# Second unit's samples issued by ACT and SyncE together, its weights fetched from the first unit's second chunk on, its transposes and splits later in the pass

## What is computed

```python
def dense(x, wi, wo):                      # D = 256, F = 1024
    return relu(x @ wi) @ wo
s0 = dense(x, swi[0], swo[0]);  s1 = dense(x, swi[1], swo[1])
h  = relu(einsum('bsd,bdf->bsf', x, wi[label]))
eo = einsum('bsf,bfd->bsd', h, wo[label])
gate_in = concatenate([eo[:, 0], s0[:, 0], s1[:, 0]], axis=-1)
w  = softmax(relu(gate_in @ g1) @ g2, axis=-1)
x  = x + eo * w[0] + s0 * w[1] + s1 * w[2]
x  = x + zX * lap_x(x) + zY * lap_y(x) + zR * x * (1 - x)
```

## Time and profile before

| | us |
|---|---|
| median of 3 runs | 1149.19 |
| lowest, highest | 1147.92, 1150.12 |
| the profiled execution | 1148.16 |
| its span, first to last instruction | 1146.6 |
| TensorE busy in it | 1136.5 |
| VectorE, ACT, GpSimd busy | 676.5, 455.3, 78.8 |

### The profile page before, as it was taken

The page is one execution under the profiler, slowest core; times in us unless marked ns, Lnnn a source line. Parts: engine busy times, 40 slices in busy tenths (PEclk is TensorE's granted clock), DMA queues, the critical chain, the costliest instruction groups (busy, mean ns, idle before and its releaser), DMA issues.

```text
span 1146.6 us, 16856 instructions
## 1 busy us (share of the span) xinstructions
PE 1136.5 (99%) x6068; PEld 970.9 (85%) x6068; DVE 676.5 (59%) x1031; ACT 455.3 (40%) x806; POOL 78.8 (7%) x123
## 2 busy tenths in 40 slices
PE   8999999999999999999999999999999999999998
PEld 7788888888888888888888888888888888888888
DVE  5556666656666644556555655565465565556556
ACT  3455555555655532323333333333333233333323
POOL 2111212211111100000000000000000000000001
PEclk9999999999999999999999999999999999999999
DMA  9555556646565514023032131231230230221200
GB/s 284 148 154 178 168 173 199 187 145 202 179 186 156 161 33 119 15 70 73 22 73 45 48 75 25 59 83 22 63 83 17 68 78 16 73 47 47 75 29 24
DMA packets 111252, 111.83 MB, mean 98 GB/s; under 512 B 78441, under 2 KB 87234, under 8 KB 111170
## 3 DMA queue, kind: packets, MB, share of 16 engines
q1 hardware_dynamic: 96802, 59.78, 19.3%
q0 software_dynamic: 13952, 50.60, 14.6%
q10 hardware_dynamic: 416, 0.39, 0.1%
HBM read 89.40 MB, written 17.04 MB: 93 GB/s over the span
## 4 chain that ended last, share of the span: by engine, by line
PE 97%; DMA 1%; SPq 1%; issue 0%; DVE 0%; DVEq 0%
PE acc L919 31%; PE hbank L892 16%; PE hbank L891 16%; PE hbank L893 16%; PE acc L920 16%; PE tbank L845 1%; DMA xs<-in_x 1%; PE acc L905 0%; SPq L1228 0%; DMA rw<-in_L_cond_swi 0%; PE hbank L870 0%; PE tbank L840 0%; PE acc L930 0%; PE acc L932 0%; PE acc L931 0%
## 5 line engine op out<-in xcount | busy, mean ns | idle before, releaser
L579 DVE SCALAR_TENSOR_TENSOR hl<-hbank,hh 128x512 fp32r<-128x512 f32 (+2 forms) x440 | 275.7, 627 | 427.9 <-ACT hh L1030 427.3
L1030 ACT ACTIVATE hh<-hbank 128x512 fp32r<-128x512 f32 (+2 forms) x440 | 240.2, 546 | 588.8 <-PE hbank L893 585.9
L919 PE MATMUL acc<-swo,hh 128*128 128x512 f32 x992 | 359.3, 396 | 0.0
L920 PE MATMUL acc<-swo,hl 128*128 128x256 f32 x992 | 277.8, 280 | 0.0
L919 PEld LDWEIGHTS acc<-swo,hh 128*128 128x128 f32 x992 | 186.3, 188 | 43.7
L891 PE MATMUL hbank<-xh,swh 128*128 128x512 f32 (+1 forms) x528 | 205.3, 389 | 0.0
L892 PE MATMUL hbank<-xl,swh 128*128 128x512 f32 (+1 forms) x528 | 205.0, 388 | 0.0
L893 PE MATMUL hbank<-xh,swl 128*128 128x512 f32 (+1 forms) x528 | 202.1, 383 | 0.0
L920 PEld LDWEIGHTS acc<-swo,hl 128*128 128x128 f32 x992 | 187.1, 189 | 9.6
L919 PE MATMUL acc<-ewo,hh 128*128 128x512 f32 x528 | 194.9, 399 | 0.3
L920 PE MATMUL acc<-ewo,hl 128*128 128x256 f32 x528 | 148.0, 280 | 0.0
(11 more groups left out here) (194 smaller groups left out, 893.2 us busy)
## 6 DMA issues: line engine op xcount, KB each, us to landing
rw<-in_L_cond_wi POOLq DMA_DIRECT2D x44, 512.0 KB, 4.5
rw<-in_L_cond_wo POOLq DMA_DIRECT2D x44, 512.0 KB, 4.7
xs<-in_x SPq DMA_DIRECT2D x128, 64.0 KB, 3.2
eo_scratch<-eo SPq DMA_DIRECT2D x128, 64.0 KB, 2.7
xs<-in_x SPq DMA_DIRECT2D x16, 512.0 KB, 4.4
rw<-in_x SPq DMA_DIRECT2D x256, 32.0 KB, 2.3
ei<-eo_scratch SPq DMA_DIRECT2D x16, 512.0 KB, 5.5
out<-ot SPq DMA_DIRECT2D x15, 512.0 KB, 6.3
```

The costliest lines, as they stand in the source:

```text
L579: e.scalar_tensor_tensor(h_slot(HL, g), bank[:, 0:w], 0.0, h_slot(HH, g).bitcast(F32), ALU.max, ALU.subtract).then_inc(h_lo, 1)
L919: e.matmul(acc[j][:, 0:2 * D], HH[:, g % NH, js], woc[:, c, :], start=(c == 0), stop=False)
L920: m = e.matmul(acc[j][:, D:2 * D], HL[:, g % NH, js], woc[:, c, 0:D], start=False, stop=last)
L1030: e.activation(h_slot(HH, g), hbank[g % HRING][:, 0:w], ACT.Relu).then_inc(h_hi, 1)
```

## The change

1. `first_samples` on ACT issues seven samples: four of the first unit, then numbers 0, 1 and 2 of the second. SP issues four of the first and numbers 3 to 7 of the second, and no longer waits for the 12th first product.
2. GpSimd waits for the 18th first product, the one of chunk `(2, 1)`, before it fetches the second unit's weights.
3. The first half of the second unit's transposes, with its splits, moves from chunk `(2, 3)` to `(2, 4)`.
4. ACT splits the second unit's pieces 0, 2, 1, 3 after chunks 4, 5, 6, 7 instead of 2, 4, 5, 7 of pass 2; VectorE follows.
5. VectorE splits the first unit's piece 0 after chunk `(1, 6)` instead of `(1, 5)`.

```diff
-FIRST_BY = {"ACT": (0, 1, 2, 3), "SP": (4, 5, 6, 7)}
+FIRST_BY = {"ACT": ((1, 0), (1, 1), (1, 2), (1, 3), (2, 0), (2, 1), (2, 2)), "SP": ((1, range(4, 8)), (2, range(3, 8)))}
@@ tile_parts(n, c)
-    if c == 3:
+    if c == (4 if n == 2 else 3):
         return [(tile, 0 if big else None)]
     return [(tile, 1)] if c == 6 and big else []
@@
-FIRST_LOW = {(1, 5): [(2, 0)], (2, 0): [(2, 2)], (2, 2): [(2, 1)], (2, 4): [(2, 3)]}
+FIRST_LOW = {(1, 6): [(2, 0)], (2, 0): [(2, 2)], (2, 2): [(2, 1)], (2, 4): [(2, 3)]}
@@ unit_cuts(n, c)
-    at = {2: 0, 4: 2} if 2 <= n < 1 + NU and UNITS[n - 2][1] == 2 else {2: 0, 4: 2, 5: 1, 7: 3}
-    out = [(n + 1, at[c])] if 2 <= n < 1 + NU and c in at else []
+    out = []
+    if 2 <= n < 1 + NU:
+        at = {4: 0, 5: 2, 6: 1, 7: 3} if n == 2 else {2: 0, 4: 2} if UNITS[n - 2][1] == 2 else {2: 0, 4: 2, 5: 1, 7: 3}
+        if c in at:
+            out.append((n + 1, at[c]))
@@ first_samples() on ACT
                 e.wait_ge(dve_seq, AT["samples"])
-                for i, b in enumerate(FIRST_BY["ACT"]):
-                    e.reg_load(regs[i], tab[0:1, 0, b:b + 1])
+                e.wait_ge(x0_prod, 1)
+                for i, (tile, b) in enumerate(FIRST_BY["ACT"]):
+                    slot = slots_of(tile - 1)[0] + b
+                    e.reg_load(regs[i % 4], tab[0:1, 0, slot:slot + 1])
...
@@ GpSimd
             e.wait_ge(h_prod, 12)
             load_unit(0, (2, 1, 3))
+
+            e.wait_ge(h_prod, 18)
             for u in range(1, NU):
                 load_unit(u, (0, 2, 1, 3))
@@ load_unit_x(u, part) on SP
                 if tile == 2:
                     e.wait_ge(x0_prod, 1)
-                    e.wait_ge(h_prod, 12)
@@ SP
-            load_unit_x(0, FIRST_BY["SP"])
-            load_unit_x(1)
+            for tile, part in FIRST_BY["SP"]:
+                load_unit_x(tile - 1, part)
```

More of the change, by code:

```diff
@@ L1066, in first_samples @@
                 e.wait_ge(dve_seq, AT["samples"])
-                for i, b in enumerate(FIRST_BY["ACT"]):
-                    e.reg_load(regs[i], tab[0:1, 0, b:b + 1])
-                    v = e.snap(regs[i], min_val=0, max_val=NS - 1)
-                    e.dma_start(XS[1][b:128:8, :, :], x[bass.ds(v, 1), :, :].rearrange("a (p j) d -> (a p) j d", p=16)) \
-                        .then_inc(x_in[1], 16)
+                e.wait_ge(x0_prod, 1)
+                for i, (tile, b) in enumerate(FIRST_BY["ACT"]):
+                    slot = slots_of(tile - 1)[0] + b
+                    e.reg_load(regs[i % 4], tab[0:1, 0, slot:slot + 1])
+                    v = e.snap(regs[i % 4], min_val=0, max_val=NS - 1)
+                    e.dma_start(XS[tile % 2][b:128:8, :, :],
+                                x[bass.ds(v, 1), :, :].rearrange("a (p j) d -> (a p) j d", p=16)) \
+                        .then_inc(x_in[tile % 2], 16)
             def quadratic(t):
```

## The result

| | before | after |
|---|---|---|
| median of 7 runs (us) | 1147.92 | 1144.82 |
| lowest, highest | 1147.42, 1150.12 | 1143.1, 1145.5 |
| span of the profiled execution | 1146.6 | 1142.8 |

The ratio after / before is 0.9967 (95% interval 0.9955 to 0.9978): 3.8 us of 1148, between 2.5 and 5.2. It compares the means of the seven runs, 1148.32 and 1144.51; the medians of the table lie 3.1 us apart. The profiled spans differ by the same 3.8 us. 4.2 us and 1145.0 were predicted. That 1144.82 lies so near to 1145.0 is in part luck: the prediction started from 1149.19, the median of three runs, and with four more runs the median before is 1147.92.

What follows compares the result with a forecast made beforehand. TensorE, busy for 99% of the span, was taken to bound the kernel. Wait 2.70 plus low clock 1.76 minus 0.3 for the first unit's samples gave 4.2 us saved: 1149.19 to 1145.0 us, range 1143.4 to 1148.0.

Steps and rivals of the forecast that it cites:

- The wait and its price: TensorE's wait at the second unit's transposes costs 2.70 us, the low clock after it 1.76 us; both go.
- The clock's term: From the second unit's transposes to the next chunk, 4.99 us at the low clock against 3.23 at full: 1.76 us.
- The samples: SyncE's last issue for the second unit comes at 20.6 instead of 24.96 and lands by 27.9.
- The shift itself is worth nothing.: Second unit's transposes moved from fourth to fifth chunk cost the same there; TensorE asks for the samples at 31.98.
- The first unit's samples: In the opening, ACT's three extra transfers delay them; 0.3 us of loss taken, between 0 and 1.9 us.
- Rival A: First unit's samples land 1.9 us later, TensorE idles 2.7 us there, the clock falls; 1148.4 us, chance 0.11.
- Slack of the weights: The second unit's first weight piece lands between 31.1 and 38.6 and may land by 40.5 without cost: zero.
- The count of the chain behind the first piece: Splits, ReLU and VectorE's work after the second unit's first weight piece take 4.0 us, due at 44.5.
- VectorE, ACT, the small loads: VectorE's fuller load, ACT's three extra issues and SyncE's small loads behind the samples each cost zero.
- B: The wait goes, but the clock still falls somewhere in the opening; 1146.8 us, chance 0.07.
- C: The second unit's samples still land last, because transfers share one set of DMA engines; 1149.2 us, chance 0.04.
- D: First unit's samples wait for the second unit's, 5.5 us of delay, and the kernel is slower; 1152.0 us, chance 0.04.

Runs made afterwards that it cites:

- the kernel without ACT's share: From the change: ACT issues only its four samples of the first unit, SyncE all eight of the second; 0.9968 of the kernel before.
- the last experiment: From the change: GpSimd waits for the 22nd first product instead of the 18th before the second unit's weights; 1.0000 of the kernel before.
- weights only: From the kernel before: only GpSimd's wait for the 18th first product and the second unit's weight splits after chunks 4 to 7; 0.9965, 1143.81 us.
- the samples only: The change with parts 2 to 5 undone: ACT issues three of the second unit's samples, SyncE five, without its wait; 0.9970, 1144.61 us.

## Why the prediction was right

- **The wait and its price.** The wait of 2.70 us and the low clock behind it went as forecast: the second unit's pass began at 44.63 (44.5 was forecast), 4.13 us earlier, at the full clock all through. The clock's term of 1.76 us was 0.16 us too large, since it set a start behind a wait against a place in a pipelined chain; by starts it is 1.60 us. Its cause is better founded now: the loss is not there without the wait, and it grows with it.
- **The samples.** Last issue at 20.6 forecast, 21.0 measured (the whole opening was 0.5 us later there: the sample table at 12.7 instead of 12.2), landing by 27.9 forecast, 27.3 measured.
- **"The shift itself is worth nothing."** True beside the other parts, but incomplete: the transposes' shift alone is worth the whole gain, and so is each other part. The prediction credited the sum to the issue of the samples; it did not ask what each part would do alone. The rows had it: samples in at 31.74, transposes asked for at 31.98.
- **The first unit's samples.** 0.3 us was taken, 0.18 us is between the two traces, and the kernel without ACT's share shows no less idle time. As far as these traces show, the term should have been zero. Their last samples, issued at 14.8 to 15.8, took no longer to land than the 4.3 to 6.0 us of the earlier trace rows:

```profile
DMA to landing us min/median/max: 4.2/4.6/5.6
```

  Rival A falls with it: the prediction reckoned up to 1.9 us for it, and 0.54 us of idle time with ACT's extra transfers against 0.69 us without them shows no such price here. The Trainium skill's rule (DMA: Bandwidth & Descriptors, Queues, rings and completion order) that each DMA engine takes turns between the queue rows that have work gives no size; these landings show no delay by it. When the transfers were put ahead of the first unit's own, the price came, 1.55 us of idle time, but by ACT's issue order.
- **Slack of the weights.** Issued at 27.77, not 26.4: the second chunk's first product ended where the next starts, at 26.55, and GpSimd issued 1.2 us after that. The first piece landed in 4.3 us, at 32.1, before ACT came to it at 34.68, so this changed nothing. The count of the chain behind the first piece was right in its places and in its 4.0 us, and left out the second piece, as the last experiment showed.
- **VectorE, ACT, the small loads.** Zero, as forecast: TensorE waits nowhere from 24 to 60 us.
- **What the sum missed.** 0.31 us at the end, where VectorE waited for a halo transfer. Before, that transfer was in ahead of TensorE's products.
- **Rivals B, C and D** did not come. B is answered by the clock's column, C by the landing at 27.3.

Of 4.2 us forecast, 3.8 were measured by ratio and by trace. Between the two traces, the clock's term was 0.16 us too large and the end took 0.31 us that the sum did not have; the opening's 0.18 us took the place of the 0.3 us.

## What to carry to other kernels

A wait has two sides, and a change can move either: ask for each part alone what it does to the time at which the thing is there, and to the time at which it is asked for; if the wait is 2.7 us and one side moves by 2.8, the other parts are spare. Price an idle stretch of TensorE with what the clock does behind it, from the same work at both levels, and take all four times as starts from one view: two views can put the same instruction 0.16 us apart, a tenth of the price here. And when slack is counted for the first of several transfers that one engine waits for in turn, count the second as well.

## What the runs showed of the hardware that was not expected

- Idle stretches of TensorE of 0.5 and 1.55 us left the granted clock full, 2.45 and 2.55 us cost 1.58 and 1.60 us at the low level, and 4.97 us cost 2.70 us.
- A 64 KB sample issued near 25 took 3.3 to 3.6 us to land when GpSimd had issued 1.5 MB of weights from 18.3 to 20.5 and held the rest back (weights only), and 6.8 to 7.3 us when it had issued 3.5 MB from 18.07 to 23.2 (the kernel before). Issued from 19.7 to 21.0, while the 1.5 MB had just been issued, it took 6.0 to 6.3 us (the change).
- The opening scatters by over 2 us from execution to execution, more than the differences looked for: the first unit's transposes start between 20.37 and 22.86, without the kernel in which ACT issues its samples in the other order (23.20). In part of the executions the first narrow matmuls are spaced 0.43 us a pair instead of 0.22, with a granted clock of 1.00 in the column. Two timelines of the same matmuls, before and with the samples only, and the stretch from 5 to 10 us of each:

```profile
5.74 0.46 PE L870 MATMUL hbank<-rx,rw 128*128 128x128 f32 x2 [0.27 <-DMA rw<-in_L_cond_swi]
```

```profile
5.71 0.77 PE L874 MATMUL hbank<-rx,rw 128*128 128x128 f32 x2
6.27 0.64 PE L875 MATMUL hbank<-rx,rw 128*128 128x128 f32 x2
```

```profile
5.00:10.00 5.00, 4.62 (x31) 4.19 (x32) 3.91 (x28) 1.37 (x5) 0.00 (x0) 1.00 1.05 373
```

```profile
5.00:10.00 5.00, 5.00 (x22) 4.82 (x23) 3.61 (x26) 1.09 (x4) 0.00 (x0) 1.00 1.05 374
```

22 matmuls instead of 31 in the same 5 us. Why it comes in some executions only was not tried.
